# Slot lists planned with one slot per partition, and a second list in five classes

## What is computed

```python
x = x + _L0_xattn_ref(_layernorm(x), ctx_2048, ...)     # img branch: 64 queries by 64 keys in each of 64 batches
x = x + _L0_ffn_ref(_layernorm(x), gate_w, w1, w2)
# in _L0_ffn_ref:
probs = softmax(x @ gate_w.T)                            # 8 experts
topw, sel = top_k(probs, 2);  topw /= sum(topw)
g, u = split(x @ w1[e].T);    out += combine[e] * ((silu(g) * u) @ w2[e].T)
```

## Time and profile before

| | us |
|---|---|
| median of 3 runs | 491.39 |
| lowest, highest run | 489.05, 491.95 |
| span of the profiled execution | 489.1 |
| busy in it: PE, DVE, POOL, ACT | 438.3, 391.4, 308.6, 276.7 |
| second stage, from the first `hst_lo` to the end | 309.6 to 489.1 |
| of it, turns of the slots | to 473.5 |

### The profile page before, as it was taken

How to read it: one execution, slowest core, us unless ns; L and a number is a source line. 1 busy time by engine, 2 the same in 40 slices (tenths; PEclk the granted TensorE clock), 3 DMA queues, 4 the chain that set the end, 5 groups by cost and what they waited for, 6 DMA issues and landing times.

```text
span 489.1 us, 15233 instructions
## 1 busy us (share of the span) xinstructions
PE 438.3 (90%) x4428; PEld 381.4 (78%) x4428; DVE 391.4 (80%) x1327; ACT 276.7 (57%) x802; POOL 308.6 (63%) x529
## 2 busy tenths in 40 slices
PE   7898999999999999898999888798999999999960
PEld 3568888888888788787888777587899999888850
DVE  7547788888888888889899787679876767898964
ACT  5355666666666566566666653454566656555630
POOL 6843458878788787876878865764344444454550
PEclk9999999999999999999999999999999999999995
DMA  6252453323323333223343324545344445879727
GB/s 207 78 161 73 137 165 88 117 86 92 104 86 112 89 91 104 81 89 100 89 118 86 88 83 105 160 155 150 99 131 121 131 125 167 271 244 294 255 98 258
DMA packets 55514, 64.62 MB, mean 132 GB/s; under 512 B 9599, under 2 KB 49034, under 8 KB 55434
## 3 DMA queue, kind: packets, MB, share of 16 engines
q1 hardware_dynamic: 44602, 42.59, 31.2%
q0 software_dynamic: 6480, 16.85, 9.7%
q10 hardware_dynamic: 4352, 4.20, 2.5%
HBM read 32.73 MB, written 23.14 MB: 114 GB/s over the span
## 4 chain that ended last, share of the span: by engine, by line
PE 41%; POOL 27%; issue 15%; DVE 13%; DMA 2%; ACT 1%; POOLq 1%; DVEq 0%; ACTq 0%; SPq 0%
POOL sorted_rows L545 8%; PE bank L1368 8%; PE bank L1369 7%; PE bank L1370 7%; PE bank L1609 4%; POOL r_qk L501 3%; POOL we_l L493 3%; POOL ct_l L487 2%; POOL rstd L501 2%; POOL row L530 2%; PE bank L1641 1%; PE bank L1642 1%; PE bank L1429 1%; PE bank L1631 1%; PE bank L1630 1%
## 5 line engine op out<-in xcount | busy, mean ns | idle before, releaser
L617 POOL DMA_INDIRECT expert_out<-probs,late x71 | 72.5, 1021 | 78.9 <-ACT probs L803 74.5
L545 POOL DMA_INDIRECT sorted_rows<-row,place_i x64 | 69.1, 1080 | 33.4 <-POOL row L537 15.6
L1368 PE MATMUL bank<-we_h,xt_h 128*128 x142 | 52.0, 366 | 2.5 <-DVE xt_l L1278 2.3
L708 ACT ACTIVATE probs<-bank 128x1024 f32<-128x1024 f32 x32 | 32.8, 1026 | 23.4 <-PE bank L1482 21.5
L791 ACT ACTIVATE xn<-bank 128x176 f32<-128x176 f32 x71 | 22.6, 318 | 41.4 <-PE bank L1370 41.4
L1369 PE MATMUL bank<-we_l,xt_h 128*128 x142 | 45.9, 324 | 0.0
L1370 PE MATMUL bank<-we_h,xt_l 128*128 x142 | 45.8, 322 | 0.0
L1288 DVE SCALAR_TENSOR_TENSOR probs<-xn,late,bank 128x128 f32<-128x128 f32 x71 | 24.4, 344 | 20.6 <-ACT xn L791 20.4
L501 POOL TENSOR_TENSOR rstd<-veps,half_neg 128x1 f32<-128x1 f32 x64 | 36.7, 573 | 5.3
L935 DVE TENSOR_REDUCE bank<-bank 128x16 f32<-128x1024 f32 x32 | 39.1, 1223 | 1.1 <-PE bank L1417 1.1
L803 ACT COPY probs<-bank 128x256 f32<-128x256 f32 x71 | 26.5, 373 | 18.9 <-PE bank L1642 16.7
(11 more groups left out here) (237 smaller groups left out, 1596.4 us busy)
## 6 DMA issues: line engine op xcount, KB each, us to landing
late<-sorted_rows SPq DMA_DIRECT2D x71, 129.0 KB, 2.2
we_f<-w_exp SPq DMA_DIRECT2D x32, 152.0 KB, 2.6
v_bd<-v_sb SPq DMA_DIRECT2D x128, 34.0 KB
ctx_in<-ctx_t SPq DMA_DIRECT2D x32, 128.0 KB, 2.7
qp<-q_hl SPq DMA_DIRECT2D x128, 32.0 KB
x<-x SPq DMA_DIRECT2D x3, 1024.0 KB, 5.9
row<-expert_out SPq DMA_DIRECT2D x6, 512.0 KB, 5.1
qp<-expert_out SPq DMA_DIRECT2D x4, 512.0 KB, 4.3
```

The lines of the kernel that those rows point to most:

```text
L545: pool.indirect_dma_start(sorted_rows, bass.IndirectOffsetOnAxis(ap=place_i[:, t.slot // 2, k, t.par:t.par + 1], axis=0), row[:, k, t.slot ...
L617: pool.indirect_dma_start(expert_out, bass.IndirectOffsetOnAxis(ap=hs(r)[:, D:D + 1].bitcast(U32), axis=0), y_sb[:, r % YRING, :], None, b ...
L1368: pe.matmul(dst, a_h, b_h, start=start, stop=False)
```

## The change

Three things change.

First, the tables `slot_no`, `region_no` and `upto` and all scratch of the planner now span 128 partitions. Partition s works out slot s alone, against 8 or 40 elements. The lists are columns: SP and PE load the register from partition `at`.

Second, there are five classes where there were three, with bounds after 16, 24, 28 and 30 tiles. `count_mid` runs three times, after attention turns 28, 32 and 34. The sums of the classes run one per turn. The list is made in turns 4 to 13.

Third, SP loads groups 12 and 13 once 63 slots are sent, group 14 once 67 are, and group 15 once all 71 are. Groups 12 to 14 use the five early buffers.

```diff
-MID = 24
+BOUNDS = (16, 24, 28, 30)
-SEGS = 3 * NE
+SEGS = CLASSES * NE
-    slot_no = sb("slot_no", [1, NSLOT], F32)
+    slot_no = sb("slot_no", [P, 1], F32)
...
-            return sp.value_load(table[0:1, at:at + 1], min_val=0, max_val=NE * REG)
+            return sp.value_load(table[at:at + 1, 0:1], min_val=0, max_val=NE * REG)
...
-            if FIN_BUF <= g < FIN_EARLY:
+            if FIN_BUF <= g < FIN_LATE:
...
-        for r in range(4):
-            sp.wait_ge(y_sent[r], 16 * ((NSLOT - 1 - r) // YRING + 1))
-        for g in range(FIN_EARLY, NT // 2):
-            load_results(g)
+        for done, low, high in zip(DONE[2:], BOUNDS[1:], BOUNDS[2:] + (NT,)):
+            for r in range(4):
+                sp.wait_ge(y_sent[r], 16 * ((done - 1 - r) // YRING + 1))
+            for g in range(low // 2, high // 2):
+                load_results(g)
...
         def place_early():
-            step(dve.tensor_tensor(past1[:, :, :], slot_no[:, 0:FULL].unsqueeze(2).to_broadcast([1, FULL, NE]),
-                                   spread(cum1[:, :], FULL, NE), ALU.is_ge))
-            stepped()
-            step(dve.tensor_tensor(past1_n[:, :, :], past1[:, :, :], spread(jump1[:, :], FULL, NE), ALU.mult))
-            step(dve.tensor_reduce(slot1[:, 0, :], past1[:, :, :], AX.X, ALU.add))
+            step(dve.tensor_scalar(past1[:, 0, :], cum1[:, :], slot_no[:, :], None, ALU.is_le))
+            stepped()
+            step(dve.tensor_tensor(past1[:, 1, :], past1[:, 0, :], jump1[:, :], ALU.mult))
...
-            if i == MID + 5:
-                count_mid()
+            if i - 4 in BOUNDS[1:]:
+                count_mid(BOUNDS.index(i - 4))
...
+        def sum_shared(a):
+            at = a * NE
+            stepped()
+            step(dve.tensor_tensor(cum2_of[:, :, :], upto[:, :, :], spread(rows2[:, at:at + NE], NE, NE), ALU.mult))
+            stepped()
+            step(dve.tensor_reduce(cum2[:, at:at + NE], cum2_of[:, :, :], AX.X, ALU.add))
+            if a:
                 stepped()
+                step(dve.tensor_scalar(cum2[:, at:at + NE], cum2[:, at:at + NE], cum2[:, at - 1:at], None, ALU.add))
 
         def place_shared():
-            step(dve.tensor_tensor(past2[:, :, :], slot_no[:, 0:SHARED].unsqueeze(2).to_broadcast([1, SHARED, SEGS]),
-                                   spread(cum2.rearrange("p a e -> p (a e)"), SHARED, SEGS), ALU.is_ge))
...
+            stepped()
+            step(dve.tensor_scalar(past2, cum2, slot_no[:, :], None, ALU.is_le))
+            stepped()
+            step(dve.tensor_tensor(past2_of[:, 0, :], past2, jump2, ALU.mult))
+            step(dve.tensor_tensor(past2_of[:, 1, :], past2, seg_w, ALU.mult))
...
-            if i == 8:
-                sum_shared()
-            if i == 9:
-                place_shared()
-            if i == 10:
-                jump_shared()
-            if i == 11:
-                rows_shared()
-            if i == 12:
-                weigh_shared()
-            if i == 13:
-                weights_shared()
-            if i == 14:
+            if 7 <= i < 7 + CLASSES:
+                sum_shared(i - 7)
+            if i == 7 + CLASSES:
+                place_shared()
+            if i == 8 + CLASSES:
                 list_shared()
```

More of the change, by code:

```diff
@@ L222, in build_in @@
     act_u = words(probs[:, :, :], "p a b -> p (a b)")[:, 4 * D:4 * D + 4 * P].rearrange("p (u n) -> p u n", u=2)
[L224 to L228, removed]
@@ L229, in build_in @@
-    past1, past1_n = (t.rearrange("p (s e) -> p s e", e=NE) for t in (past1, past1_n))
+    row1, w1, row2, w2, first, rest_at, seg_w, mid_i = pieces(late[:, KEEP:], 1, 1, 1, 1, NE, SEGS, SEGS, NE)
+    used, whole = (rest_at[:, a * NE:(a + 1) * NE] for a in range(2))
+    row1, w1, row2, w2, mid_i = (t.bitcast(I32) for t in (row1, w1, row2, w2, mid_i))
+    past1, cum1_of, counts1_i, counts1, cum1, jump1, slot1 = pieces(
+        late[:, KP_END:KEEP], 2 * NE, NE * NE, 2 * NE, 2 * NE, NE, NE, 3)
@@ L1109, in spread @@
         def spread(t, rows, cols):
-            return t.unsqueeze(1).to_broadcast([1, rows, cols])
+            return t.unsqueeze(1).to_broadcast([P, rows, cols])
         def count_early():
@@ L1114, in count_early @@
             for a, more in enumerate((0.0, P - 1.0)):
-                step(dve.scalar_tensor_tensor(counts1_i[:, a, :], filled[0:1, :], more, region_no[:, :],
+                step(dve.scalar_tensor_tensor(counts1_i[:, a, :], filled[:, :], more, region_no[:, :],
                                               ALU.add, ALU.subtract))
@@ L1221, in count_shared, with count_whole @@
+            step(dve.tensor_tensor(rows2[:, 0:SEGS - NE], rest_at[:, NE:SEGS], rest_at[:, 0:SEGS - NE], ALU.subtract))
             step(dve.memset(base2[:, SEGS:SEGS + 1], float(NE * REG)))
+            step(dve.scalar_tensor_tensor(base2[:, 0:SEGS].rearrange("p (a e) -> p a e", a=CLASSES),
+                                          rest_at.rearrange("p (a e) -> p a e", a=CLASSES), float(P),
+                                          spread(region_no[:, :], CLASSES, NE), ALU.mult, ALU.add))
+        def count_whole():
@@ L1228, in count_shared, with rows_shared @@
             step(dve.tensor_copy(whole2, count2_i))
-            step(dve.tensor_tensor(jump2, base2[:, 1:SEGS + 1], base2[:, 0:SEGS], ALU.subtract))
+        def rows_shared():
             stepped()
-            step(dve.tensor_tensor(rows2[:, 2 * NE:SEGS], whole2, whole_mid, ALU.subtract))
+            step(dve.tensor_tensor(rows2[:, SEGS - NE:SEGS], whole2, rest_at[:, SEGS - NE:SEGS], ALU.subtract))
             stepped()
-        def sum_shared():
-            for a in range(3):
-                step(dve.tensor_tensor(cum2_of[:, a, :, :], upto[:, :, :], spread(rows2[:, a * NE:(a + 1) * NE], NE, NE),
-                                       ALU.mult))
@@ L1254, in jump_shared, with list_shared @@
             stepped()
-        def weigh_shared():
-            step(dve.tensor_tensor(past2_of[:, :, :], past2[:, :, :], spread(seg_w, SHARED, SEGS), ALU.mult))
+            step(dve.tensor_tensor(past2_of[:, 0, :], past2, jump2, ALU.mult))
+            step(dve.tensor_tensor(past2_of[:, 1, :], past2, seg_w, ALU.mult))
+        def list_shared():
             stepped()
-        def rows_shared():
-            step(dve.tensor_reduce(slot2[:, 0, :], past2_of[:, :, :], AX.X, ALU.add))
+            step(dve.tensor_reduce(slot2[:, 0:2], past2_of[:, :, :], AX.X, ALU.add))
```

100 lines of the change are left out of this document (44 added, 56 removed).

## The result

The changed kernel takes **485.43 us** (median of 4 runs, 483.04 to 486.03), the kernel before, run beside it, 491.48 us (489.05 to 491.95, 4 runs). The ratio is 0.9873, 95% interval [0.9838, 0.9907]: faster, by 1.3% (0.9 to 1.6). The forecast was 483.5 us, the range 479.6 to 487.4. The profiled execution took 485.2 us and its span is 483.5; before, the span was 489.1.

The account below looks back on a forecast made before the run. DVE was taken to set the pace in second-stage turns 9 to 13, and its adds the last five groups' row at the end. -3.5 - 4.2 - 0.2 = -7.9 us gave 483.5 us from the median, range 479.6 to 487.4.

Parts of the forecast that it names:

- Turns 8 to 17: Second stage: planner's long passes on DVE removed, -4.7 + 1.2 = -3.5 us, between -4.7 and -1.9.
- The end: After the last slot: three groups' adds leave the row, -4.0 - 0.3 + 0.1 = -4.2 us, between -5.5 and -3.2.
- POOL's hold on the short steps: Turns 8 to 13: POOL operations hold DVE's short steps, 1.0 us charged; as a rival, nearly all held, 487.4 us, chance 0.12.
- My rate of two in six: Turns 6 to 14 before: two of six short DVE steps caught by POOL, applied to seven: 0.7 us, taken as 1.0.
- The length of a sum: Second stage, DVE: product, reduction and addition for one class take 0.61 us, less 0.08 overlap, 0.53, against 0.59 to spare.
- The end's small terms: After the last slot: lone last load 3.8 us, a gain of 0.3; stores delay the last result by 0.1 us.
- the end gives back half: Rival: stores and last result share DMA engines, chain after 474.75 2 us longer, end worth -2.2, 485.5 us; chance 0.11.
- The loads of groups 12 to 14 at nothing: Late second stage: these groups load 1.5 MB while slots still run, costed at nothing.
- The first stage: Cheaper early planner steps against two more counts, one hidden: -0.57 - 0.1 + 0.43 = -0.2 us; stage moves by 1.35 either way.
- The register loads from another partition: Rival: PE and SP reading partition `at` pay more per load; at 0.3 us each, 505 us, slower; chance 0.04.
- The sum and the median: Whole kernel: -3.5 - 4.2 - 0.2 = -7.9 us, 481.2 from the profiled span, 483.5 from the median.

Follow-up runs that it names:

- the waiting stores: The changed kernel, but ScalarE issues the stores of groups 12 to 14 only after the last result has landed: 484.76 us, ratio 0.9882.
- The pair with fillers: The kernel before and the changed kernel, each with filler matmuls at three places where PE idles: 490.29 us and 483.31 us.
- the changed kernel on its second chip: The changed kernel run again with nothing altered, beside the kernel before: 483.61 us against 491.37, ratio 0.9854.

## Why the prediction was right

**The bound, and the two parts.** Both places were read rightly. Turns 8 to 17: forecast 18.4 to 20 us, measured 18.87 (and 18.8 to 19.2 in all the others with the new planner); -3.5 was forecast, -4.2 came. The end: -4.2 forecast, -4.1 came. That the end agrees to 0.1 us is luck: two of its terms were off by 0.3 and 0.4 us, in opposite directions (below).

**POOL's hold on the short steps** was the term that was too dear. I charged 1.0 us; none of the seven steps of turns 8 to 13 was held. It was not that they missed POOL: three of the four class additions and the last clamp start inside one of its operations. One addition in DVE's time, and POOL's operation beside it, in the changed kernel:

```profile
339.57 0.23 DVE L1243 TENSOR_SCALAR ctx_in<-ctx_in 128x8 f32<-128x8 f32 x1
```

```profile
339.18 0.97 POOL L614 DMA_INDIRECT expert_out<-probs,late  x1 [1.21 <-ACT probs L800]
```

It takes 0.23 us, as the one at 332.90 us that had no POOL beside it (POOL's ended at 332.79). A copy of `count_whole` was held, in a turn that is hidden, and it ended with POOL's operation, at 326.40:

```profile
325.95 0.45 DVE L1226 CAST ctx_in<-ctx_in 128x8 f32<-128x8 int32 x1
```

```profile
325.43 0.97 POOL L542 DMA_INDIRECT sorted_rows<-row,place_i  x1 [0.31 <-ACT probs L800]
```

So the copy agrees with the lock of the Trainium skill's "SBUF — State Buffer" (engine and AXI ports), and the additions don't, as I had applied it: one input tensor and a POOL operation under way are not enough. The 11 profiles with the new planner say the same. Of their 40 class additions 38 began inside a POOL operation, and none took more than 0.25 us; the copy in turn 5 began inside one in all 11, was held to its end in nine (0.39 to 0.45 us), and took 0.17 us in two. What sets the additions apart from the one that was held before, on one partition, and the nine copies from the two, the runs don't show: it stays open. My rate of two in six, from six cases, was no forecast for the next seven.

**The length of a sum** was too cheap: 0.53 us forecast, 0.78 measured. The product, the reduction and the addition take 0.23, 0.22 and 0.23 us where I had 0.18, 0.21 and 0.16, and the next `hst_lo` starts 0.26 us after the addition does, so nothing of it overlaps. Little of that is the 128 partitions. The kernel before has this same addition, which takes its number from a tensor, a second time in turn 8, not held:

```profile
331.97 0.22 DVE L1244 TENSOR_SCALAR ctx_in<-ctx_in 1x8 f32<-1x8 f32 x1
332.23 0.42 DVE L1278 TENSOR_TENSOR xt_l<-bank,xt_h 128x256 fp32r<-128x256 f32 x1
```

It takes 0.22 us on one partition, and there too the next `hst_lo` starts 0.26 us after it. So 0.16, the length of a plainer step, was the wrong row, the overlap of 0.08 us isn't there, and the held one had lost 0.26 us and not 0.33. The sum is 0.18 us over what the turn could give, 4 or 5 times, less what later turns won back. The two errors have opposite signs: +0.5 us over the undisturbed pace instead of +1.2.

**The end's small terms** were wrong both ways as well. The last load takes 3.46 us (3.21 to 3.60 in the six profiles of this order, each with the store of group 14 beside its first microsecond): I had chosen 3.8, the least of the 16 there were the earlier trace rows, which all had company. The estimate from the Trainium skill ("DMA: Bandwidth & Descriptors", cost components), 3.2 us, would have been nearer to the shortest of them. The last result was delayed by 0.53 us and not 0.1; the waiting stores show that it was the stores. The rival "the end gives back half" had the right mechanism, at a fourth of its price.

**The loads of groups 12 to 14 at nothing** is the step that failed. They, or something that comes with them, move the last start back by 0.7 us: PE's register load stands in their way. My question had been whether SP's queue or a buffer would be late; I did not ask which other small transfer is in a row there.

**The first stage**: forecast -0.2 with +-1.35. `place_early` went from 0.95 us to two steps of 0.20 and 0.17, and the four turns with the planner from 37.71 to 37.05; the count behind turn 32 costs 0.49 us where 0.43 was forecast. From the 20th maximum to the last `bn_aggr` that makes 114.35 us against 114.93.

**The register loads from another partition** cost nothing. The waits of turns 4 to 17 in the changed kernel (us in total, times, longest), for those of the earlier trace rows:

```profile
PEld bank L1592 <- issue: 1.8, 7, 0.4
PE bank L1592 <- issue: 0.4, 2, 0.2
```

Together 2.2 us, nine times, as before.

**The sum and the median.** -7.9 us was forecast. The pair with fillers gives -7.0 and -7.1, the changed kernel on its second chip -7.8, on its first -6.1. There its profiled execution lost 2.8 us in the start, 2.4 of them to the clock; how many of the other three runs did is not known, so why the first pair shows less stays open. I also misread the profile's own time: the runs take 1.7 us more than their span (485.2 and 483.5), so the profiled execution of before was one of some 490.8 us and not the lowest of the three, 489.05. The forecast, set from the median, did not depend on it.

## What to carry to other kernels

Where a planner's small steps run on an engine that sets the pace, count the whole dependent row, each step at the length that a step of the same form has in the trace, and compare it with the idle time of one turn: here 0.78 us against 0.59 still cost something, though each step looked free. When work is taken out of the last row, ask which transfers now run beside the last result, and name the small ones, register loads too. Before a difference between two profiles is explained, look at the granted clock of each stretch, and profile the same kernel a second time: 2.8 us here were the execution's own, 2.4 of them the clock's.

## What the runs showed of the hardware

- The granted clock falls to its 1.2 GHz level at the same few places, but not in every execution. Read in stretches of four microseconds it was 0.50 at 40 to 44 us in one profile of 13 (the fall lasted from 38 to 45 us and cost 2.4 us; it didn't come in the same program's next profile), 0.57 to 0.66 at 12 to 16 us in three, 0.57 to 0.67 at 294 to 298 in three, and 0.59 to 0.76 at 316 to 320 in five. PE had been idle for 2.32 us ahead of the fall at 40, and for 2.18 and 2.02 us at the same place in two profiles where the clock stayed at 1.00.
- A few filler matmuls at 40, 294 and 318 us: none of the four profiles with them shows a fall there. The highest run came down from 495.2 to 491.9 us and from 487.4 to 483.9 in two pairs, and stayed in the third (485.4, 485.3); the medians moved by 1.1, 0.3 and 0.3 us.
- A register load from SBUF on PE is not of fixed length: 0.30 us in the middle of each kernel's, but 0.8 to 1.46 us for one to five of the last 35 in every profile, while results are loaded for the groups (1.17 us in the kernel before, 1.26 in the changed one, 1.7 us behind the issue of two loads of 512 KB).
- The last load of 512 KB takes 3.46 us, and 4.42 beside three stores of 256 KB; a result of one slot 2.10 us alone, 2.63 beside those stores, 3.73 and 3.94 where all three stores and the loads ahead of them fall closer together.
- A DVE addition on 8 elements whose number comes from a tensor takes 0.22 us on one partition and 0.23 on 128.
